# One 128-row slot fewer in a routed expert layer, and another order for the shared tiles behind it

## The reference

```python
x = x + tanh(g_xattn[0]) * xattn(layernorm(x), ctx, ...)      # 16 heads, 4 key/value heads
y = layernorm(x)                                              # 4096 tokens, 256 wide
probs = softmax(y @ w_router); top_v, top_i = top_k(probs, 2) # 8 experts, two for each token
routed[t] = 2.5 * sum over the two experts e of share[t,e] * ((silu(y @ w_gate[e]) * (y @ w_up[e])) @ w_down[e])
shared = (silu(y @ ws_gate) * (y @ ws_up)) @ ws_down          # inner width 352; 176 in an expert
x = x + tanh(g_ffn[0]) * (routed + shared)
```

## Time and profile before

| | us |
|---|---|
| median of 3 runs | 1246.29 (1243.81 to 1246.75) |
| the profiled execution, its own time | 1244.25 |
| its span, first to last instruction | 1242.5 |
| mean granted TensorE clock | 0.989 of full speed |
| PE busy over the span | 1198.6 |
| DVE, POOL, ACT busy | 1018.0, 928.3, 887.4 |

### The profile page before, as it was taken

How to read it: one execution, slowest core, us unless ns; L and a number is a source line. 1 busy time by engine, 2 the same in 40 slices (tenths; PEclk the granted TensorE clock), 3 DMA queues, 4 the chain that set the end, 5 groups by cost and what they waited for, 6 DMA issues and landing times.

```text
span 1242.5 us, 31522 instructions
## 1 busy us (share of the span) xinstructions
PE 1198.6 (96%) x8828; PEld 1143.2 (92%) x8829; DVE 1018.0 (82%) x3016; ACT 887.4 (71%) x3758; POOL 928.3 (75%) x1122
## 2 busy tenths in 40 slices
PE   1699999999999999999999999999999999999998
PEld 1599999999999999999999999999999999999997
DVE  8888888888888888888888888888888677777443
ACT  7777777777777777777777777777777546666322
POOL 2687888878888888888888888888887425556654
PEclk8799999999999999999999999999999999999999
DMA  6623332333222222323333333322236536554574
GB/s 167 206 74 113 106 104 92 99 107 107 89 89 89 89 89 93 89 93 92 95 112 110 98 101 115 106 75 74 74 108 210 192 102 188 166 165 145 181 243 145
DMA packets 128981, 148.78 MB, mean 120 GB/s; under 512 B 13856, under 2 KB 108448, under 8 KB 128160
## 3 DMA queue, kind: packets, MB, share of 16 engines
q1 hardware_dynamic: 122400, 130.29, 34.9%
q0 software_dynamic: 6528, 17.90, 3.8%
HBM read 67.26 MB, written 80.89 MB: 119 GB/s over the span
## 4 chain that ended last, share of the span: by engine, by line
PE 94%; DVE 2%; issue 1%; ACT 1%; DMA 1%; SPq 0%; POOL 0%; DVEq 0%; POOLq 0%; ACTq 0%
PE b_kv L1632 15%; PE b_o L1683 14%; PE b_q L1618 14%; PE b_sc L1657 9%; PE b_aT L1672 9%; PE b_pT L1665 5%; PE b_qT L1646 4%; PE b_kv L1884 3%; PE b_q L1884 3%; PE b_kT L1642 2%; PE b_q L1700 2%; PE b_aT L1813 2%; PE b_kT L1700 2%; PE b_aT L1901 1%; PE b_pT L1901 1%
## 5 line engine op out<-in xcount | busy, mean ns | idle before, releaser
L1632 PE MATMUL b_kv<-w_group,kv_in_hi 128*128 128x256 f32 x1024 | 214.0, 307 | 0.5 <-DVE k_sin L1200 0.5
L1618 PE MATMUL b_q<-w_group,kv_in_hi 128*128 128x512 f32 x512 | 173.0, 419 | 22.5 <-DVE q_sin L1214 13.9
L708 POOL TENSOR_TENSOR qk_r<-qk_me,minus_half 128x6 f32<-128x6 f32 x128 | 173.8, 1358 | 10.0
L916 ACT ACTIVATE probs<-b_sc,neg_max 128x128 f32<-128x128 f32 x512 | 180.6, 373 | 0.5 <-DVE neg_max L1224 0.5
L1632 PEld LDWEIGHTS b_kv<-w_group,kv_in_hi 128*128 128x128 f32 x1024 | 169.2, 192 | 8.0 <-issue 1.2
L712 POOL TENSOR_TENSOR q_rot<-q_rot,q_sin 128x512 f32<-128x512 f32 x128 | 164.7, 1287 | 6.5 <-DVE q_sin L1214 1.5
L1683 PE MATMUL b_o<-wo_hi,aT_hi 128*128 128x256 f32 x512 | 153.1, 299 | 0.1
L910 ACT ACTIVATE pT<-b_pT 128x512 f32<-128x512 f32 x128 | 76.7, 599 | 104.2 <-PE b_pT L1665 102.3
L1632 PE MATMUL b_kv<-w_group,kv_in_lo 128*128 128x256 f32 x512 | 145.1, 283 | 0.0
L1683 PE MATMUL b_o<-wo_lo,aT_hi 128*128 128x256 f32 x512 | 141.8, 277 | 0.0
L1683 PE MATMUL b_o<-wo_hi,aT_lo 128*128 128x256 f32 x512 | 141.6, 276 | 0.0
(11 more groups left out here) (267 smaller groups left out, 3988.5 us busy)
## 6 DMA issues: line engine op xcount, KB each, us to landing
xs_scratch<-zeros SPq DMA_DIRECT2D x34, 1032.0 KB, 6.3
s_in<-xs_scratch SPq DMA_DIRECT2D x72, 129.0 KB, 2.3
yT_scratch<-yT SPq DMA_DIRECT2D x32, 256.0 KB, 2.0
yS<-yT_scratch SPq DMA_DIRECT2D x32, 256.0 KB, 3.3
routed<-ys_scratch SPq DMA_DIRECT2D x32, 256.0 KB, 3.6
w_hi_all<-w_scratch SPq DMA_DIRECT2D x3, 1536.0 KB, 13.5
x_in<-in_x SPq DMA_DIRECT2D x32, 128.0 KB, 2.3
ctx_raw<-in_ctxT SPq DMA_DIRECT2D x32, 128.0 KB, 2.6
```

The source lines that it names most:

```text
L708: nc.gpsimd.tensor_tensor(qk_r[g % 2][:], qk_me[:], minus_half[:, 0:REP + NB], ALU.pow).then_inc(r_ready, 1)
L916: last = nc.scalar.activation(probs[:, j, :], b_sc[:, j * P:(j + 1) * P], ACT.Exp, bias=neg_max[g % 2][:, j:j + 1], accum_out=row_sum[g % ...
L1618: last = nc.tensor.matmul(b_q[:], kv_in[p][a][:, c, 1:3, :], wq_of(b, gg)[:, c, :], start=(c == 0 and (a, b) == PASSES[0]), stop=(c == DC ...
L1632: last = nc.tensor.matmul(b_kv[:, s * 2 * HD:(s + 1) * 2 * HD], kv_in[p][a][:, c, 2 * s:2 * s + 2, :], wkv_of(b, c)[:, g % KVH, :], start= ...
```

## The change

1. **A slot fewer.** `USED` = 71. Slot 71, which holds no token whatever the router picks, is neither loaded, computed nor scattered; every loop body's last group and the waits on the counts are cut to match. On PE the first transposition of slot 71, its gate and up, second transposition and down go.
2. **The joint.** Between the last slots and tile 8 PE now does: second transposition of slot 70, gate of tile 8, down of slot 69, up of tile 8, down of slot 70, transposition of tile 8.
3. **Late tiles.** Four result banks (`b_sc`, `b_kv`, `b_aT`, `b_pT`), two pairs of `hT`, and `add_shared` of tile t-3 instead of t-2 between `hid` and `hT_lo` of tile t. ACT waits for down of t-2 instead of t-1, PE for `shared_ready` of t-4 instead of t-2.
4. **Down.** Its nine matmuls run pass by pass over the three row chunks, not chunk by chunk over the three passes. The six that need only `hT_hi` wait for `hT_hi` alone, and the other three for `hT_lo`. This holds for all 32 shared tiles.
5. **The last tile.** The three low matmuls of tile 30 stand behind the transposition of tile 31.
6. **SP.** A tile is stored one round of the queue later, and the last tile's store is now behind that of tile 7, no longer ahead of it.
7. **Tile 3.** DVE makes `hT_lo` of tile 3 ahead of the steps that count the rows of each expert, not in their middle.

```diff
+USED = (TOPK * B * S + E * (P - 1)) // P
...
-        hT = parts("hT", [P, FC, P], turn_at)
+        hT = [parts(f"hT{p}", [P, FC, P], turn_at) for p in range(2)]
...
-        b_late = (b_q, b_kT, b_o, b_aT), (b_q, b_kT, b_o, b_pT)
+        b_late = [(b_q, b_kT, b_o, y) for y in (b_sc, b_kv, b_aT, b_pT)]
...
-                        sp.wait_ge(st_ys[q], 16 * (SLOTS // QUAD))
+                        sp.wait_ge(st_ys[q], 16 * ((USED - q + QUAD - 1) // QUAD))
...
-                sp.wait_ge(shared_ready, t + 1)
-                store_out(t)
+                if t > EARLY:
+                    sp.wait_ge(shared_ready, t)
+                    store_out(t - 1)
             while early < EARLY:
                 sp.wait_ge(x1_mixed, MIX_ORDER.index(early) + 1)
                 store_out(early)
                 early += 1
+            sp.wait_ge(shared_ready, TILES)
+            store_out(TILES - 1)
...
                 act.wait_ge(hT_done, t + 1)
-                need(act, y_done, t)
+                need(act, y_done, t - 1)
...
-            slot_hidden_hi(SLOTS - 1, 1)
-            slot_out(SLOTS - 2, SLOTS // QUAD - 1, 2)
+            slot_hidden_hi(USED - 1, 0)
             silu_gate(EARLY)
-            slot_out(SLOTS - 1, SLOTS // QUAD - 1, 3)
+            slot_out(USED - 2, SLOTS // QUAD - 1, 1)
+            slot_out(USED - 1, SLOTS // QUAD - 1, 2)
...
                 hidden(t)
-                if t > EARLY + 1:
+                if t > EARLY + 2:
+                    add_shared(t - 3)
+                if t == TILES - 1:
                     add_shared(t - 2)
                 hidden_lo(t)
...
-            def shared_down(t):
-                pe.wait_ge(hT_lo, t + 1)
-                need(pe, shared_ready, t if t < EARLY else t - 1)
+            def shared_down_part(t, a, b):
                 for c in range(FC):
                     rows = min(P, FS - c * P)
...
+            def shared_down_hi(t):
+                pe.wait_ge(hT_hi, t + 1)
+                need(pe, shared_ready, t if t < EARLY else t - 3)
+                for a, b in PASSES[:2]:
+                    shared_down_part(t, a, b)
+
+            def shared_down_lo(t):
+                pe.wait_ge(hT_lo, t + 1)
+                shared_down_part(t, *PASSES[2]).then_inc(y_done, 1)
...
-            slot_hidden_T(SLOTS - 1, 1)
-            slot_down(SLOTS - 2, 0, expert_down[1])
-
-            pe.wait_ge(s_hid_ready, SLOTS - 1)
-            pe.wait_ge(sT_lo, SLOTS)
-            shared_gate_up(EARLY)
-            slot_down(SLOTS - 1, 1, expert_down[2])
+            slot_hidden_T(USED - 1, 0)
+            shared_gate(EARLY)
+            slot_down(USED - 2, 1, expert[1])
+            shared_up(EARLY)
+            slot_down(USED - 1, 0, expert[2])
             shared_hidden_T(EARLY)
-            pe.wait_ge(s_out_ready, SLOTS - 1)
             for t in range(EARLY + 1, TILES):
                 shared_gate_up(t)
-                shared_down(t - 1)
-                shared_hidden_T(t)
+                if t == EARLY + 3:
+                    pe.wait_ge(s_out_ready, USED)
+                if t < TILES - 1:
+                    shared_down(t - 1)
+                    shared_hidden_T(t)
+            shared_down_hi(TILES - 2)
+            shared_hidden_T(TILES - 1)
+            shared_down_lo(TILES - 2)
             shared_down(TILES - 1)
```

More of the change, by code:

```diff
@@ L49 @@
 SPARE = SLOTS - TOPK * TILES
+USED = (TOPK * B * S + E * (P - 1)) // P
+assert USED == SLOTS - 1
 MANY = 3 * QUAD
@@ L388, in banks @@
         def banks(t):
-            return b_early[t % 2] if t < EARLY else b_late[t % 2]
+            return b_early[t % 2] if t < EARLY else b_late[t % 4]
         def w2_piece(t, part):
@@ L616, in slots @@
                 for q in range(QUAD):
-                    load_slot(QUAD * k + QUAD + q, q)
+                    if not (isinstance(k, int) and QUAD * k + QUAD + q == USED):
+                        load_slot(QUAD * k + QUAD + q, q)
                     if late is not None and q % 2 == 1:
@@ L822, in slots @@
                     m = MANY * k + o
-                    if last and o >= MANY - AHEAD:
+                    if last and o == MANY - 1:
+                        continue
+                    if last and o >= MANY - 1 - AHEAD:
                         pool.wait_ge(s_out_ready, m + 1)
@@ L1039, in hidden_hi @@
                 act.wait_ge(hT_done, t + 1)
-                need(act, y_done, t)
-                nc.scalar.activation(hT[HI][:].rearrange("p c n -> p (c n)"), banks(t)[2][:, 0:FW], ACT.Copy) \
+                need(act, y_done, t - 1)
+                nc.scalar.activation(hT[t % 2][HI][:].rearrange("p c n -> p (c n)"), banks(t)[2][:, 0:FW], ACT.Copy) \
                   .then_inc(hT_hi, 1)
@@ L1090, in slots @@
                     m, p = QUAD * k + q, q % 2
+                    if last and q == QUAD - 1:
+                        continue
                     slot_silu(m, p)
@@ L1095, in slots @@
                         slot_hidden_hi(m - 1, 1 - p)
-                    if not (last and q >= QUAD - 2):
+                    if not (last and q >= QUAD - 3):
                         slot_hi(m + 2, p)
@@ L1365, in hidden_lo @@
                 dve.wait_ge(hT_hi, t + 1)
-                nc.vector.tensor_tensor(hT[LO][:].rearrange("p c n -> p (c n)"), banks(t)[2][:, 0:FW],
-                                        hT[HI][:].rearrange("p c n -> p (c n)").bitcast(F32), ALU.subtract) \
+                nc.vector.tensor_tensor(hT[t % 2][LO][:].rearrange("p c n -> p (c n)"), banks(t)[2][:, 0:FW],
+                                        hT[t % 2][HI][:].rearrange("p c n -> p (c n)").bitcast(F32), ALU.subtract) \
                   .then_inc(hT_lo, 1)
@@ L1492, in _ @@
             add_shared(2)
+            hidden_lo(3)
             def then(ins):
@@ L1581, in slots @@
                         slot_hidden_lo(m - 1, 1 - p)
-                    if not (last and o >= MANY - 2):
+                    if not (last and o >= MANY - 3):
                         slot_lo(m + 2, p)
@@ L1805, in shared_hidden_T, with shared_down @@
                 last.then_inc(hT_done, 1)
-            def shared_down(t):
-                pe.wait_ge(hT_lo, t + 1)
-                need(pe, shared_ready, t if t < EARLY else t - 1)
+            def shared_down_part(t, a, b):
                 for c in range(FC):
                     rows = min(P, FS - c * P)
[L1812 to L1816, removed]
+                    last = nc.tensor.matmul(banks(t)[3][:, 0:D], hT[t % 2][a][0:rows, c, :], wd_s[b][0:rows, c, :],
+                                            start=(c == 0 and (a, b) == PASSES[0]),
+                                            stop=(c == FC - 1 and (a, b) == PASSES[-1]))
+                return last
+            def shared_down_hi(t):
[6 more added lines that the diff above has]
+                shared_down_part(t, *PASSES[2]).then_inc(y_done, 1)
+            def shared_down(t):
+                shared_down_hi(t)
+                shared_down_lo(t)
             T2, T1, LAST = TILES - 2, TILES - 1, 4 * TILES - 1
```

3 lines of the change are left out of this document (1 added, 2 removed).

## The result

| | before | after |
|---|---|---|
| median of the runs, us | 1245.73 (7 runs, 1243.81 to 1246.75) | 1241.4 (7 runs, 1240.48 to 1242.11) |
| profiled execution, us | 1244.25 | 1241.4 |
| its span, us | 1242.5 | 1239.6 |

The ratio is 0.9964, with a 95% interval of 0.9955 to 0.9974: 4.33 us or 0.36% faster. 1241.0 was forecast. Close as this is, the sum behind it was not right. Two of its five terms, 1.17 us together, are not on the path that sets the end, a third came true for another reason than the one given, and what does set the end, POOL's last additions and the row with which POOL closes the block, is not in the sum. Moving that out of the way brought 2.9 us more.

The account below looks back on a forecast made before the run. PE was taken to bound the kernel, so only fewer matmuls or fewer gaps help. Terms 2.55 + 1.09 + 0.76 + 0.41 + 0.52 = 5.33 us, taken from the median 1246.29, gave 1241.0 us, range 1238.6 to 1244.0.

Parts of the forecast that it names:

- Slot and joint: PE from the last slots to tile 9: dropping slot 71 and rebuilding the joint with tile 8 saves 2.55 us.
- Stall at tile 10: PE's wait for tile 10's hT_lo, behind tile 8's addition, goes in full with additions three tiles late: 1.09 us.
- End of the last tile: Tile 31: earlier transposition, 0.17, and down starting once the high half is ready, 0.59, save 0.76 us together.
- Last store: SP at the end: tile 7's store is issued earlier, beside PE's work, so the last issue comes 0.41 us earlier.
- Early tiles: Down of tiles 6 and 7 no longer waits for the low half: 0.26 us each, 0.52 together.
- At tile 3, counted 0: Tile 3's earlier hT_lo only changes places with steps for the table of slots: 0, between -0.5 and +0.6 us.
- Order of passes: Down's nine matmuls in new order, with a wait already met, cost 0 within 0 to 0.09 us a tile.
- the 3.35 from which the sum was to be wrong: Sign in the late tiles: gate to gate over 3.35 us, against 3.32 expected, would prove the sum wrong.
- the rival: Down's new pass order is slower: 0.09 us for each changed weight, nine in each of 32 tiles, 1267 us; chance 0.04.
- the wait in each tile is paid: Rival: PE pauses where down's low matmuls begin, up to 0.09 us in each of 32 tiles, 1243.9 us; chance 0.14.
- the order of passes: Rival: changed weights make down's new order slower, 26 us over 32 tiles, 1267 us; chance 0.04.
- the stall only moves: Rival: tile 8's addition blocks hT_lo of tile 11 instead, so the 1.09 us stays, 1242.1 us; chance 0.06.

Follow-up runs that it names:

- the slot alone: The kernel before with its 72nd slot left out in every engine and nothing else changed: 1243.34 us, 0.9985 of before.
- the addition two behind: The changed kernel with DVE's addition of a late tile two tiles behind instead of three, run twice: 1240.58 us and 1240.39 us.
- the run with one wait: The changed kernel with each shared tile's down waiting for both halves at once, pass order kept, last tile as before the change: 1244.05 us.
- the two comparisons: The changed kernel against the kernel before, measured twice, the second time on another chip: 1241.4 us (ratio 0.9964) and 1242.86 us (0.9965).
- the first four experiments: The changed kernel with routed loads one place earlier, 1238.49 us; four more POOL additions, 1243.78; old last tile and store order, 1242.07; early loads plus these, 1241.99.

## Why the prediction was right, and where it wasn't

Term by term, as forecast and as measured:

- **Slot and joint, 2.55:** measured 2.62 (2.78 - 0.16), of which 1.77 come with the slot alone and 0.85 with the new joint. Building the joint from pieces of like shape gave 5.96 for 5.93.
- **Stall at tile 10, 1.09:** measured 1.07, but the reason given was wrong. I took the 5.51 us behind the last scatter as fixed and let the later additions make room for it. They are 4.3 to 4.5 in every version without slot 71, and the stall goes without later additions (the slot alone, the addition two behind). Nothing in my rows pointed to that; the 1.09 was right by luck. That the later additions cost nothing was the worse step. Against before that is true, since SP waits for one tile less; against leaving them out, they hold POOL's end back by one tile.
- **End of the last tile, 0.76:** measured 0.78 on PE (4.44 - 3.66). **Last store, 0.41:** measured 0.13 (4.57 - 4.44), because SP first had to issue the store of tile 7, which waited for POOL's mix until 1233.51. Neither moves the end of the changed kernel. The step that failed is the reading of the last stretch: I followed the chain of waits, which ends with `x_most` at 1238.07, and filled the 4.4 us from there to the end of the span with a store of 0.82 and a landing of 1.7, without asking what ran in the rest.
- **Early tiles, 0.52:** 0.52 by the run with one wait. At tile 3, counted 0, a wait of 0.35 for `hT_lo` gave way to one of 0.34 for `s_pair`; from its gate to the transposition of `s_pair` PE takes 3.92 us instead of 4.02, a gain of 0.10.
- **Order of passes, 0 within 0 to 0.09 a tile:** 0.010 a tile, 0.2 us in the late tiles. The gates stayed under the 3.35 from which the sum was to be wrong. That is 0.001 a matmul, and not the 0.09 of the rival, which also counted nine changed weights a tile where only three were new: the old order changed the rows of `hT` six times in nine already. The Trainium skill (TensorE: Matmul & The Clock Gate, LDWEIGHTS) has a load cost by its columns alone. The trace of the kernel before agrees: a load of the short third chunk, 96 rows by 128 columns, shows 192 ns, and one of 128 by 128 shows 190.

Add up what lies on POOL's path: the early tiles, slot and joint, the stall and the order of passes, 0.62 + 2.62 + 1.07 - 0.19 = 4.1. The medians of the two comparisons gave 4.3 and 4.7. (0.62 is the 0.16 of the table and 0.46 by which the attention stage ended later in this execution; that place differs by up to 1.8 us between two traces of one kernel.) The forecast had 1.17 for the last tile and the last store, which the end didn't show, and so 1.0 us too much in its sum (5.33 against 4.33). Of this 0.56 was offset by the start: the three runs that I started from had a median of 1246.29, seven had 1245.73. That the forecast was met within 0.4 us is luck to that extent.

The rivals: "the wait in each tile is paid" and "the order of passes" came out at a tenth of a microsecond or two; "the stall only moves" didn't happen. The one that was missing is "the end is not where the chain of waits ends".

## What to carry to other kernels

Account for every microsecond between the end of the chain of waits and the end of the span: look at each engine's last rows, its drain too, before pricing anything in the last tile. When two edits shift a wait in opposite directions, price each alone; here one was worth some 2 us, about half of what the whole change brought, and the other gave it back. And when one transfer takes a microsecond longer in one version than in another, look for a packet of an instruction queue in its way before looking for a reason in the edit.

## What the runs showed of the hardware

- POOL's drain at the end of the block takes 5.9 to 6.0 us from the end of its last addition, in every trace; ACT's and DVE's take 0.5, the one of PE's weight loads 0.8 to 1.4, SP's 0.007. It is the same whether POOL finished 7 us ahead of the end or last of all, so here it is a fixed tail of POOL. POOL's last work was an addition in all of them; another last instruction was not tried.
- The last 256 KB of routed rows took 2.7 to 4.1 us from SP's issue to POOL's addition. In four traces a packet of `q8 instruction` lies on this way, and there it is 3.3 to 4.1; in the nine others it is 2.7 to 3.2. For the first load it is 4.0 in the two traces with such a packet and 2.7 to 2.9 in the eleven without. On a path that ends the kernel this is a spread of 1 us between executions.
- From gate and up of slot 2 to those of slot 70 PE takes 135.6 to 135.7 us in the trace of the changed kernel and in those of the first four experiments, which ran together; in the six later traces, from other chips, it takes 137.6 to 139.0. The kernel before, to slot 71, has 137.7 in its first trace and 139.6 in its later one. These 2 us or more are most of what the groups of runs differ by, whatever the kernel. Most of it is one place: in all seven later traces the step of one slot, which begins between 1119 and 1122 us, takes 3.1 to 3.9 us instead of 2.0, with waits of PE for `s_hid` and `s_hT_lo`. Its cause was not looked for.
